# First layer of a two-layer kernel: more value buffers, values in halves, product and scan in SBUF, sums of tiles on TensorE

## The reference, cut to what matters

```python
cross = jnp.einsum('bnw,hw->bhn', x, k1) + p1
diag  = jnp.einsum('bnw,hw->bhn', x, k2)
extra = jnp.einsum('bnw,hw->bhn', x, k3)
values = jnp.einsum('bnw,hwa->bhna', x, value_weight)
cross, diag, extra = (cexp(cross), cexp(diag), cexp(extra))   # exp of the clipped value
num = jnp.cumsum(cross * values, axis=2) * p2e * extra + values * diag
den = jnp.cumsum(cross, axis=2) * p2e * extra + diag
out = num / den
return jnp.einsum('bhna,hwa->bnw', out, output_weight)
```

## Time and profile before

| | |
|---|---|
| time, median of 3 runs | 2427.04 us (2421.03 to 2428.21) |
| the profiled execution | 2423.78 us, span 2421.7 us |
| TensorE matmul busy | 2072.6 us (86%) |
| VectorE busy | 1894.7 us (78%) |
| ACT busy | 1456.9 us (60%) |
| GpSimd busy | 602.0 us (25%) |
| mean granted clock of TensorE | 0.939 |

### The profile page before, as it was taken

One profiled execution on the slowest core, in us unless ns is written; L12 is line 12 of the kernel. 1 busy time (PEld: TensorE's weight loads), 2 busy tenths in 40 slices (PEclk: granted clock), 3 DMA queues, 4 the chain that ended last, 5 costly groups with the idle time before them and its releaser, 6 DMA issues.

```text
span 2421.7 us, 49342 instructions
## 1 busy us (share of the span) xinstructions
PE 2072.6 (86%) x18320; PEld 1204.0 (50%) x18320; DVE 1894.7 (78%) x3719; ACT 1456.9 (60%) x3090; POOL 602.0 (25%) x480
## 2 busy tenths in 40 slices
PE   5997899787799699978779969987788996998877
PEld 4675233556467423364647733336464772334645
DVE  7746998887765699878776579987877558998786
ACT  4333698748334379784733438967563344996765
POOL 2632000332252200124134310031504330004050
PEclk9999799999899789999989979999998996999999
DMA  4001200100000210101000031010100003001010
GB/s 159 1 1 53 55 12 11 30 21 19 19 1 1 77 33 9 21 21 32 16 10 1 1 86 27 9 30 12 33 14 9 1 1 93 20 12 34 5 34 22
DMA packets 63896, 63.28 MB, mean 26 GB/s; under 512 B 22000, under 2 KB 49200, under 8 KB 63152
## 3 DMA queue, kind: packets, MB, share of 16 engines
q1 hardware_dynamic: 60472, 57.27, 9.4%
q10 hardware_dynamic: 3192, 2.90, 0.4%
HBM read 24.68 MB, written 15.01 MB: 16 GB/s over the span
## 4 chain that ended last, share of the span: by engine, by line
PE 52%; DVE 22%; ACT 17%; issue 5%; DMA 2%; SPq 1%; POOL 0%; DVEq 0%; ACTq 0%
PE PS L1412 50%; ACT arena L765 9%; DVE arena L1150 3%; DVE arena L1260 2%; ACT arena L708 2%; DVE s_at L1235 1%; DVE arena L1228 1%; PE PS L1430 1%; DMA tmp<-xf 1%; DVE tmp L1235 1%; ACT arena L773 1%; DVE arena L1353 1%; ACT arena L733 1%; ACT arena L735 1%; ACT x_in L779 1%
## 5 line engine op out<-in xcount | busy, mean ns | idle before, releaser
L1412 PE MATMUL PS<-arena 128*32 128x256 f32 (+5 forms) x11328 | 788.8, 327 | 115.2 <-DVE arena L1150 24.2
L1412 PEld LDWEIGHTS PS<-arena 128*32 128x32 f32 (+5 forms) x11328 | 349.1, 118 | 554.0 <-ACT arena L708 203.0
L1150 DVE TENSOR_REDUCE arena<-PS 128x2 f32<-128x1024 f32 x512 | 592.5, 1216 | 29.5 <-PE PS L1412 28.3
L708 ACT ACTIVATE arena<-PS 128x512 f32<-128x512 f32 x944 | 513.2, 596 | 93.2 <-PE PS L1412 69.5
L661 ACT ACTIVATE arena<-PS 128x512 f32<-128x512 f32 x256 | 150.7, 597 | 244.2 <-PE PS L1412 244.1
L1412 PEld LDWEIGHTS PS<-w2e,arena 128*128 128x128 f32 x2048 | 246.0, 192 | 50.7 <-issue 49.8
L1113 DVE TENSOR_TENSOR arena<-PS,arena 128x512 f32<-128x512 f32 x128 | 86.2, 688 | 208.5 <-PE PS L1412 208.1
L1412 PE MATMUL PS<-w2e,arena 128*128 128x128 f32 x2048 | 247.7, 275 | 0.3
L765 ACT ACTIVATE arena<-PS,arena 128x128 f32<-128x128 f32 x512 | 236.5, 626 | 0.0
L511 POOL TENSOR_TENSOR zz<-zz,arena 128x512 f32<-128x512 f32 x104 | 135.2, 1300 | 265.6 <-DVE arena L1113 236.7
L1412 PE MATMUL PS<-wqkv,arena 128*128 128x512 f32 x384 | 176.8, 598 | 21.7 <-ACT arena L747 21.7
(11 more groups left out here) (308 smaller groups left out, 3301.1 us busy)
## 6 DMA issues: line engine op xcount, KB each, us to landing
arena<-arena SPq DMA_DIRECT2D x120, 128.0 KB, 2.3
scr_q<-arena SPq DMA_DIRECT2D x40, 128.0 KB, 2.4
scr_k<-arena SPq DMA_DIRECT2D x40, 128.0 KB, 2.4
arena<-scr_k SPq DMA_DIRECT2D x24, 200.0 KB
arena<-scr_q SPq DMA_DIRECT2D x24, 192.0 KB
scr_m<-arena SPq DMA_DIRECT2D x256, 1.0 KB
x_in<-in_x SPq DMA_DIRECT2D x5, 512.0 KB, 4.5
arena<-scr_m SPq DMA_DIRECT2D x128, 2.0 KB
```

The costliest lines, as they stand in the source:

```text
L708: act.activation(pb[:, n % 8, HALF * r:HALF * r + HALF], PS[:, (2 * n + r) % 3, :], ACT.Exp)\
L1150: dve.tensor_reduce(mxp[:, blk % 2, 2 * s:2 * s + 2, t, hf], PS[:, at:at + 2, :], AX, ALU.max)\
L1412: return pe.matmul(o, w, v, start=start, stop=stop, **kw)
```

## The change

Four buffers for values take the place of two, and chunks 1 and 3 are written to banks 6 and 7, which are free until the first `out_product`. The first four chunks are filled ahead of the loop; the other four are issued as eight halves of 512 tokens, put before `out_product` or behind bx by two tables. The product is written to `sm` in SBUF, and the scan runs in place there, so x of the next chunk waits for the product alone. The copy of `bsb` for chunk 0 comes from banks 0 and 1. The tile sums `rsum` are gone: the denominator is accumulated from eight matmuls. The router matmuls move behind the bx of the last chunk. `qk3`, a tile of the second layer, gets a fixed place in `arena`.

```diff
+VALS = 4
+HALVES_BEFORE = (0, 1, 1, 1, 1, 1, 1, 0)
+HALVES_AFTER = (0, 0, 1, 0, 1, 0, 0, 0)
+V_BEFORE, V_AFTER = {2: 4, 3: 5, 6: 7}, {4: 6}
...
-        rsum = take([T, H0])
...
-        vsb = take([2, N])
+        vsb = take([VALS, N])
...
-        qk3 = take([2, 3, N], BF16, route_end)
+        qk3 = take([2, 3, N], BF16, 12288)
...
+        def value_bank(c):
+
+            return 6 if c in (1, 3) else 0
...
                     act.wait_ge(S["v_ps"], c + 1)
+                    if c >= VALS:
+                        act.wait_ge(S["cv"], c - VALS + 1)
+                        act.wait_ge(S["ub"], c - VALS + 1)
+                    act.copy(vsb[:, c % VALS], pair(value_bank(c))).then_inc(S["vsb"], 1)
+
+                def move_b(c):
+
+                    act.wait_ge(S["bx_ps"], c + 1)
                     if c >= 2:
-                        act.wait_ge(S["cv"], c - 1)
                         act.wait_ge(S["ub"], c - 1)
-                    act.copy(vsb[:, c % 2], pair(0)).then_inc(S["vsb"], 1)
+                    act.copy(bsb[:, c % 2], pair(4 if c else 0)).then_inc(S["bsb"], 1)
...
-                act.wait_ge(S["bx_ps"], 1)
-                act.copy(bsb[:, 0], pair(6)).then_inc(S["bsb"], 1)
+                move_b(0)
                 move_v(1)
                 move_v(2)
-                for c in range(1, CH):
-                    act.wait_ge(S["bx_ps"], c + 1)
-                    if c >= 2:
-                        act.wait_ge(S["ub"], c - 1)
-                    act.copy(bsb[:, c % 2], pair(4)).then_inc(S["bsb"], 1)
-                    if c + 2 < CH:
-                        move_v(c + 2)
+                move_b(1)
+                move_v(3)
+                for c in range(1, CH - 1):
+                    if c in V_BEFORE:
+                        move_v(V_BEFORE[c])
+                    move_b(c + 1)
+                    if c in V_AFTER:
+                        move_v(V_AFTER[c])
...
-                link(dve.memset(rsum[:, 0], 0.0))
-                for t in range(T - 1):
-                    ins = dve.tensor_tensor(rsum[:, t + 1], rsum[:, t], cross[:, t], ALU.add)
-                    if t < T - 2:
-                        link(ins)
-                ins.then_inc(S["rs"], 1)
...
-                    dve.tensor_tensor(pair(2), vsb[:, c % 2], pair(2), ALU.mult).then_inc(S["cv"], 1)
+                    dve.tensor_tensor(sm[:, c % 2], vsb[:, c % VALS], pair(2), ALU.mult).then_inc(S["cv"], 1)
                     dve.wait_ge(S["cv"], c + 1)
-                    dve.tensor_tensor_scan(sm[:, c % 2], ones[:, 0:1].broadcast_to([P, N]), pair(2), 0.0,
+                    dve.tensor_tensor_scan(sm[:, c % 2], ones[:, 0:1].broadcast_to([P, N]), sm[:, c % 2], 0.0,
                                            ALU.mult, ALU.add).then_inc(S["sm"], 1)
...
+                def value_half(i):
+
+                    c, hf = i // 2, i % 2
+                    if c == 1:
+                        pe.wait_ge(S["xrT"], 2)
+                    elif c == 2:
+                        pe.wait_ge(S["bsb"], 1)
+                    elif c:
+                        pe.wait_ge(S["vsb"], c - 1 if c == 3 else c)
+                    ins = mm(PS[:, value_bank(c) + hf, :], res["vw"][:, P * c:P * c + P], xT[:, HALF * hf:HALF * hf + HALF])
+                    if hf:
+                        ins.then_inc(S["v_ps"], 1)
...
-                values(0)
+                pe.wait_ge(S["ex"], 1)
+                den = PS[:, 5, 0:T * H0].rearrange("p (t h) -> p t h", h=H0)
+                mm(den, upper[:], ex[:, :, 0:16], stop=False)
+                for t in range(1, T):
+                    ins = mm(den[:, t:T], ones[:], ex[:, 0:T - t, 0:16], start=False, stop=(t == T - 1))
+                ins.then_inc(S["den_ps"], 1)
...
-                pe.wait_ge(S["rs"], 1)
-                mm(PS[:, 5, 0:T * H0], upper[:], ex[:, :, 0:16], stop=False)
-                mm(PS[:, 5, 0:T * H0], ones[:], rsum, start=False).then_inc(S["den_ps"], 1)
+                value_half(0)
+                value_half(1)
                 pe.wait_ge(S["c3T"], 1)
                 spread(2, 0, cross3T, 0, "x_ps")
-                values(1)
+                value_half(2)
...
+                value_half(3)
                 pe.wait_ge(S["ab3T"], 1)
-                pe.wait_ge(S["xrT"], 2)
-                spread(6, 64, AB3T, 0, "bx_ps")
+                pe.wait_ge(S["vsb"], 1)
+                spread(0, 64, AB3T, 0, "bx_ps")
+                spread(4, 0, AB3T, 0, "ax_ps")
+                pe.wait_ge(S["cv"], 1)
+                spread(2, 0, cross3T, 1, "x_ps")
+                value_half(4)
+                value_half(5)
+                pe.wait_ge(S["t1"], 1)
+                spread(4, 64, AB3T, 1, "bx_ps")
+                value_half(6)
+                value_half(7)
...
+                half = 8
+                for c in range(1, CH - 1):
+                    pe.wait_ge(S["cv"], c + 1)
+                    spread(2, 0, cross3T, c + 1, "x_ps")
+                    pe.wait_ge(S["bsb"], c + 1)
                     spread(4, 0, AB3T, c, "ax_ps")
...
+                    for _ in range(HALVES_BEFORE[c]):
+                        value_half(half)
+                        half += 1
+                    out_product(c - 1)
+                    pe.wait_ge(S["t1"], c + 1)
+                    spread(4, 64, AB3T, c + 1, "bx_ps")
+                    for _ in range(HALVES_AFTER[c]):
+                        value_half(half)
+                        half += 1
+                pe.wait_ge(S["vsb"], CH)
+                for t in range(T):
+                    ins = mm(PS[:, 1, 12 * t:12 * t + 12], xr0T[:, P * t:P * t + P], res["w_route"][:])
+                ins.then_inc(S["rt"], 1)
+                pe.wait_ge(S["bsb"], CH)
+                spread(4, 0, AB3T, CH - 1, "ax_ps")
```

More of the change, by code:

```diff
@@ L245, in build @@
         hg = take([3, N])
-        names = """out_gone xnT_ps xnT lg clipped ex c3 c3T_ps c3T rs den_ps ab ab3 ab3T_ps ab3T v_ps vsb x_ps cv sm bx_ps bsb ax_ps t1 ub o s_ps s
+        names = """out_gone xnT_ps xnT lg clipped ex c3 c3T_ps c3T den_ps ab ab3 ab3T_ps ab3T v_ps vsb x_ps cv sm bx_ps bsb ax_ps t1 ub o s_ps s
         xr xrT_ps xrT rt rt_read rt_in rt_ex up_ps hs y ym z g0 xn2
@@ L499, in _ @@
                         pool.wait_ge(S["o"], c - 1)
-                    pool.tensor_tensor(ub[:, c % 2], vsb[:, c % 2], bsb[:, c % 2], ALU.mult).then_inc(S["ub"], 1)
+                    pool.tensor_tensor(ub[:, c % 2], vsb[:, c % VALS], bsb[:, c % 2], ALU.mult).then_inc(S["ub"], 1)
                 pool.wait_ge(S["s"], T)
```

27 lines of the change are left out of this document (3 added, 24 removed).

## The result

| | before | after |
|---|---|---|
| median, us | 2427.62 (4 runs, 2421.03 to 2431.78) | 2469.38 (4 runs, 2464.50 to 2471.18) |
| ratio, 95% interval | | 1.0171, 1.0151 to 1.0191 |
| span of the profiled execution, us | 2421.7 | 2467.2 |
| mean granted TensorE clock | 0.939 | 0.936 |

What follows compares the result with a forecast made beforehand. TensorE, VectorE and GpSimd were within 10% at 5.24 us a chunk; exclusion would make the shared path 6.7. Four stretches of 64.9 us plus 0.9, less 241.86, gave +18.6 on 2427, about 2445; range 2422 to 2464.

Steps and rivals of the forecast that it cites:

- The step that decides: Scan in SBUF and GpSimd's operations fully exclude each other, giving 6.7 us a chunk instead of 5.24.
- The loop's length: From product 0 at a to the last oT add's end at a+54.1, with 6.7 us a chunk from scan 1 on.
- its race: Scan 1 and GpSimd's add of chunk 0 come within 0.16 us; if the scan wins, 1.9 us a stretch better.
- The opening: Denominator passes replace rsum: 2.1 us, 3.3 in the third stretch; ab3 1.3 us earlier, product 1 5.6 us earlier.
- the lower clock of 652 to 665: TensorE's slow spell in the second stretch's opening before the change; predicted not to recur, as TensorE is busy nearly throughout.
- The end: From the last oT add to the first down 3.6 us as before; the add's 4.2 us delay is passed on whole.
- The route matmuls: Moved behind bx of the last chunk, they end 2.4 us after its start, before scan 7 ends: priced at nothing.
- The sum: Four stretches of 64.9 us plus 0.9, less 241.86: +18.6 us, about 2445; as rival A, chance 0.68.
- The range: 2422 to 2464 us, taking in rivals A, C and D; A's own range was 2436 to 2460.
- Rival C: In the loop, exclusion idles TensorE 1.4 us or more a chunk, its clock falls: +4 each stretch, 2461; chance 0.10.

Runs made afterwards that it cites:

- GpSimd light: Changed kernel with GpSimd's product and sum, and VectorE's last add, on 64 of 1024 columns, scan still in SBUF: 2414.93 us, ratio 0.9948 to the kernel before.
- the kernel with values first: Changed kernel with the value product of chunk 0 moved ahead of the 16 accumulated sum passes, nothing else: 2456.62 us, ratio 1.0123 to the kernel before.
- the filled kernel: Changed kernel with four extra calls (eight matmuls, results unread) on TensorE behind the last spread of each stretch: 2489.24 us, ratio 1.0260 to the kernel before.

## Why the prediction was right in kind and wrong in size

**The step that decides: right.** The scan with two SBUF inputs and GpSimd's operations exclude each other, broadcast or not. The prediction said 6.7 us a chunk; the sums stand 6.61 apart. It said a mean of 4 us for the scans of chunks 1 to 7 (3.6 measured, (110.0 - 4 x 2.29) / 28: scan 1 was hardly held, 2.33 to 2.38, and scan 2 in part, 3.33) and sums up to 4.5 (4.16). The rule that the prediction takes from the Trainium skill ("SBUF — State Buffer", Who interferes with whom) holds for this scan too: held in the changed kernel and in the kernel before with that part alone, not held with the scan in PSUM or GpSimd light.

**The loop's length: close by luck, two errors that cancel.** From product 0 to the last sum's end the prediction had 54.1 us; measured are 57.4, 53.8, 55.8 and 55.3, and 53.7 in three of the four stretches of the kernel with values first. The order it described is not the one that came: scan 1 won its race in all four stretches, which the prediction held possible and priced at 1.9 us less; from then on GpSimd's sum of chunk k - 1 stands behind scan k, and at the end two GpSimd operations are left instead of one, 2.2 us more; a chunk is 0.1 us shorter, 0.6 in all. That makes the 53.8 of the second stretch. Where the lower clock held up `bsb` 0 (first and third) chunk 1 came 2.0 us later, and where the route matmuls met it (first and fourth) the last sum came some 1.6 us later: 53.8 + 2.0 + 1.6 = 57.4, 53.8 + 2.0 = 55.8, 53.8 + 1.6 = 55.4, the measured values within 0.1. Over four stretches this term was 5.9 us too small.

**The opening: wrong, the term taken at the wrong end of its bounds.** The step says "I take 2.1 us here and 3.3 us in the third" for the passes, and has values 0 done "before a"; its own upper bound was +2.6 us a stretch. Product 0 was forecast 6.1 to 7.2 us after Exp and came at 9.55, 8.83, 9.55 and 9.21: 11.6 us later in all, and past even the upper bound (8.7) in every stretch. The cause is the clock: passes of 3.6 us, then values 0 of 3.06 to 3.78, which now stand in the critical path. The granted clock of the passes is 0.50 in stretches 2 to 4; for the first the profile shows 1.00, but the durations are the same. Two stretches of the filled kernel met the higher clock in the same instructions and started product 0 at 6.36 and 6.61, so the working was right for the clock it assumed. "TensorE is also busy nearly throughout, so the lower clock of 652 to 665 should not recur" failed with it: it recurred in the opening and at the end. The order that puts the passes ahead of values 0 costs 12.8 us in this kernel and showed no cost with GpSimd light, where product 1 came at 14.7 us at the latest (16.3 here).

**The end: wrong, a term put at nothing.** "Behind it ... 3.6 us to the first `down` as before" and "TensorE's own path (out_product, up, out_product) ends earlier": measured are 6.17, 6.32, 6.38 and 6.25 us, 10.7 us more in all. TensorE's path ended later. In the second and third stretch `out_product` 6 could start only when GpSimd's sum of chunk 6 ended (711.27), 2.1 us after the last scan; in the first and fourth it was later still, behind the slow route matmuls. It and `up` took some 8 us at the lower clock instead of 5.5. "The route matmuls, moved behind bx of the last chunk, end 2.4 us after its start, before scan 7 ends: nothing" is the same step's other half: with the scan in PSUM, where no sum is late, `out_product` 6 still took 3.6 us and 5.2 us passed from sum to `down`, 1.6 a stretch more than the 3.6. In the first and fourth stretch of the changed kernel these matmuls were not even done when scan 7 ended: they ended 3.9 us after it.

**The sum.** Counted from Exp to `down`: 18.6 + 11.6 + 5.9 + 10.7 = 46.8 us, against 47.0 measured (284.6 - 237.6). The windows, which end at `up`, show 45.9.

**The range.** It took the bound of the clock once, for the opening, as +8 of a range that ended at 2464, and had no case in which TensorE sets the end of the stretch: with the end's 10.7 us it would have reached 2475, past the 2469 measured. (Its lower end, 2436, is 2 us below its own sum, 2427 + 11.) Rival C (the clock, 0.10) looked for the fall in the loop for idle time of 1.4 us a chunk. There `out_product` kept 2.05 us through chunks 0 to 4, and chunk 5 too in two stretches; the fall came at both ends. In other kernels whose scan is held C's fall did come inside the loop: in the kernel before with the scan in SBUF, with the old opening and, in one stretch, with values first.

**Left open.** Why the granted clock of the opening is the lower one in one execution's stretch and the higher in another's with the same instructions: scan 1 of kernels with the old opening and the scan in PSUM starts at 16.0 in some and at 17.8 to 18.3 in others, some 2 us a stretch. The differences among the kernels near 2425 us are of that size. Open is also what besides the place of the route matmuls decides the fall at the end, and what brings it inside the loop in some stretches only.

## What to carry to other kernels

Before an operand is moved from PSUM to SBUF to free a bank, look what GpSimd does at that time: if the VectorE instruction then reads two SBUF operands, add its duration to GpSimd's and compare the sum with the engine that paces the loop (here 2.3 + 4.7 = 7.0, 6.6 after overlaps, against 5.3). A delay of the second product was paid in full in the held loop and in the light one, and so is every operation left over at the end, so the last iteration has to be followed to the next stage for each engine, with the work that still waits in GpSimd's queue. Where a trace shows one stretch at the higher clock and its neighbours at the lower, price each new TensorE item at both and keep both ends in the range.

## What the runs showed of the hardware that was not expected

- A scan whose first operand is one broadcast column counts as two SBUF inputs for the exclusion: 2.29 us alone, up to 4.4 beside GpSimd. The waiting side's duration grows; no idle time appears in the trace.
- GpSimd waits as well: its sum took 4.16 us each time in the changed kernel, its product 4.34 in the kernel before with the scan in SBUF, 2.35 otherwise.
- In the changed kernel with eight more TensorE matmuls a batch, the first transposes of the next batch started 4.3 us later, with no releaser (9.4 to 9.7 us idle instead of 5.1). In the other kernels, among them one with the same eight matmuls, it stayed at 5.1. The cause was not traced.
- With the scan in PSUM and the old opening, `out_product` 6 took 2.96 to 3.62 us where 16 matmuls of 12 columns and a wait of 1.1 us lay ahead of it, and 2.05 in all four stretches with the same wait but the narrow matmuls behind it.
